# Keys of the first block handled in two stages, and the last four windows of turned keys split by VectorE

## The reference, cut to what matters

```python
q = layernorm(x) @ Wq + bq                      # 1024 x 128
k, v = ctx @ Wk + bk, ctx @ Wv + bv             # 6404 x 128
x = x + tanh(g_xattn) * softmax(q @ k.T / sqrt(128)) @ v
n = layernorm(x)
w = softmax(n @ Wr + br); keep the two largest of 8, divide by their sum
x = x + tanh(g_ffn) * sum_e w_e * (relu(n @ W1_e + b1_e) @ W2_e + b2_e)
```

## Time and profile before

| what | us |
|---|---|
| median of three executions | 283.12 |
| lowest and highest | 281.38, 283.39 |
| the profiled execution, its own time | 283.62 |
| span of its profile | 281.5 |
| TensorE busy | 269.8 |
| VectorE busy | 208.7 |
| ScalarE busy | 187.9 |
| GpSimd busy | 112.2 |

### The profile page before, as it was taken

How to read it: one execution, slowest core, us unless ns; L and a number is a source line. 1 busy time by engine, 2 the same in 40 slices (tenths; PEclk the granted TensorE clock), 3 DMA queues, 4 the chain that set the end, 5 groups by cost and what they waited for, 6 DMA issues and landing times.

```text
span 281.5 us, 5083 instructions
## 1 busy us (share of the span) xinstructions
PE 269.8 (96%) x1667; PEld 247.4 (88%) x1667; DVE 208.7 (74%) x415; ACT 187.9 (67%) x339; POOL 112.2 (40%) x147
## 2 busy tenths in 40 slices
PE   7988999999999999999999799998999899999994
PEld 7765899999999999999899799997899798999994
DVE  4795789966378987889737578777587688466796
ACT  2891665556566665565667698887554655799991
POOL 3796799647700020000000643870015443457530
PEclk9997999999999999999999999999999999999999
DMA  6600002000089100000000222344300111214212
GB/s 202 250 0 2 0 3 77 2 0 0 2 234 338 36 0 2 1 0 3 0 0 2 68 81 77 113 121 136 99 20 21 37 31 29 87 36 105 78 46 84
DMA packets 18485, 17.08 MB, mean 61 GB/s; under 512 B 2410, under 2 KB 14940, under 8 KB 18460
## 3 DMA queue, kind: packets, MB, share of 16 engines
q1 hardware_dynamic: 17372, 15.31, 17.9%
q0 software_dynamic: 640, 1.31, 1.7%
q10 hardware_dynamic: 448, 0.14, 0.2%
HBM read 13.34 MB, written 3.42 MB: 60 GB/s over the span
## 4 chain that ended last, share of the span: by engine, by line
PE 55%; issue 23%; DVE 10%; POOL 6%; DMA 3%; ACT 2%; POOLq 0%; DVEq 0%; ACTq 0%
DVE pmax L910 5%; PE ps L1265 4%; PE ps L1354 4%; PE ps L1355 4%; PE ps L1356 4%; PE ps L1332 4%; PE ps L1333 4%; PE ps L1334 4%; POOL x_slots L649 3%; PE ps L1213 3%; PE ps L1442 3%; PE ps L1467 2%; PE ps L1469 2%; PE ps L1468 2%; PE ps L1506 2%
## 5 line engine op out<-in xcount | busy, mean ns | idle before, releaser
L817 ACT ACTIVATE ex_hi<-ps 128x768 fp32r<-128x768 f32 (+1 forms) x78 | 57.0, 730 | 60.8 <-PE ps L1334 60.0
L1100 DVE TENSOR_TENSOR ex_lo<-ps,ex_hi 128x768 fp32r<-128x768 f32 (+2 forms) x67 | 59.1, 882 | 27.0 <-ACT ps L821 24.1
L910 DVE TENSOR_REDUCE pmax<-ps 128x1 f32<-128x512 f32 (+2 forms) x92 | 63.7, 731 | 12.8 <-PE ps L1265 11.8
L821 ACT ACTIVATE ps<-ps 128x768 f32<-128x768 f32 (+2 forms) x67 | 50.3, 750 | 0.0
L1332 PE MATMUL ps<-q_hi,ctxT_hi 97*128 97x384 f32 (+1 forms) x153 | 49.9, 326 | 0.0
L1354 PE MATMUL ps<-ex_hi,ctx_both 128*97 128x384 f32 (+1 forms) x153 | 49.8, 325 | 0.0
L1333 PE MATMUL ps<-q_lo,ctxT_hi 96*128 96x384 f32 (+1 forms) x153 | 49.1, 321 | 0.0
L1334 PE MATMUL ps<-q_hi,ctxT_lo 96*128 96x384 f32 (+1 forms) x153 | 48.7, 318 | 0.0
L1355 PE MATMUL ps<-ex_hi,ctx_both 128*96 128x384 f32 (+1 forms) x153 | 48.6, 318 | 0.0
L1356 PE MATMUL ps<-ex_lo,ctx_both 128*97 128x384 f32 (+1 forms) x153 | 48.6, 318 | 0.0
L547 POOL TENSOR_TENSOR rstd<-veps,minus_half 128x3 f32<-128x3 f32 (+1 forms) x6 | 5.0, 829 | 88.7 <-DVE veps L897 88.7
(11 more groups left out here) (212 smaller groups left out, 533.1 us busy)
## 6 DMA issues: line engine op xcount, KB each, us to landing
raw<-in_ctx_dram SPq DMA_DIRECT2D x6, 384.0 KB, 5.8
w_raw<-in_L_ffn_W_dram SPq DMA_DIRECT2D x8, 256.0 KB, 3.9
raw<-in_L_ffn_W_dram SPq DMA_DIRECT2D x8, 256.0 KB, 5.9
raw<-in_L_ffn_b_dram SPq DMA_DIRECT2D x8, 256.0 KB, 3.5
shared<-routing SPq DMA_DIRECT2D x8, 192.0 KB, 3.1
x_slots<-shared SPq DMA_DIRECT2D x1, 1088.0 KB, 6.3
y_slots<-shared SPq DMA_DIRECT2D x17, 64.0 KB, 1.5
shared<-in_L_ffn_b_dram SPq DMA_DIRECT2D x1, 512.0 KB, 3.5
```

The source lines that it names most:

```text
L817: nc.scalar.activation(ex_pair(ex_hi, u % P_RING, js, n), scores, ACT.Exp)
L821: nc.scalar.activation(whole, scores, ACT.Exp).then_inc(ex_ready, 1)
L910: nc.vector.tensor_reduce(pmax[:, FIRST_TILE[b] + t, place:place + 1], max_home(s)[:, 0:w], AX.X, ALU.max).then_inc(max_reduced, 1)
L1100: nc.vector.tensor_tensor(ex_pair(ex_lo, u % P_RING, js, n), whole, ex_pair(ex_hi, u % P_RING, js, n).bitcast(F32), ALU.subtract).then_inc ...
```

## The change

The maxima of block 0 are found in two stages. Stage one covers the first 3072 keys: 6 slots of 1024 keys at the start, and units 0 to 11 use the row of their maxima. The other 3332 keys make 14 slots of 512 keys (the last two of 260) beside units 2 to 9 of block 0; the second row is the maximum of those keys and zero, is kept in a copy of the query (`q_second`) and used by units 12 to 25. The slots of block 1 move to units 10 to 23 of block 0. The sums of stage two go to the other half of the bank; both halves are projected in turn (two more matmuls, in unit 7 of block 1), and VectorE joins them with the factor exp(`drop`), where `drop` is the difference of the two rows. The steps behind move by one or two units. Windows 9 to 12 of the turned keys (chunks 36 to 50) are turned behind the first slots into banks 5, 6, 7 and 5, copied once by ScalarE and split by VectorE from PSUM. GpSimd's order changes, and it makes the low part of exp for units 14 to 25. The transposes whose results are not read around `turn_max(0)` are gone.

```diff
-WARM_MAX = 12
-WARM_ROW = 5
...
-POST_FIRST = dict(u_copy=3, project=5, gate=5, residual=6, stats=7, turn=12, logits=14, shift=15, compare=16, exp=17,
+POST_FIRST = dict(u_copy=3, project=5, first_copy=6, project_second=7, gate=7, residual=8, stats=9, turn=13, logits=14, shift=15, compare=16, exp=17,
...
-POOL_LO_FROM = 15
+POOL_LO_FROM = 14
+
+STAGE_UNITS = 12
+SECOND_ROW_UNIT = 11
+TURNED_BY_VECTOR = 9
...
+    STAGE_KEY = 2 * STAGE_UNITS * P
...
+    PASS = [2 * BANK] + [BANK] * (ROUNDS - 1)
...
+    SLOTS = [(r, t, key, min(PASS[r], ROUND_KEYS[r][1] - key), ROUND_AT[r] + w)
+             for r in range(ROUNDS) for w, key in enumerate(range(*ROUND_KEYS[r], PASS[r])) for t in range(BLOCK_TILES[ROUND_BLOCK[r]])]
+    SLOTS_UNTIL = [sum(PLACES[k] * BLOCK_TILES[ROUND_BLOCK[k]] for k in range(r + 1)) for r in range(ROUNDS)]
...
+    ROUND_UNITS = {1: (0, 2, SECOND_ROW_UNIT - 2), 2: (0, SECOND_ROW_UNIT - 1, MAX_UNIT), 3: (1, 0, MAX_UNIT)}
...
+        for r, (block, first, last) in ROUND_UNITS.items():
+            if block == b and first <= i <= last:
+                n, units = SLOTS_UNTIL[r] - SLOTS_UNTIL[r - 1], last + 1 - first
+                return range(SLOTS_UNTIL[r - 1] + (i - first) * n // units, SLOTS_UNTIL[r - 1] + (i - first + 1) * n // units)
+        return []
+
+    def round_of(b, i):
+        return b + 1 if b or i >= STAGE_UNITS else 0
...
-        QK_UNIT = {1: 0, 2: 6}
+        QK_UNIT = {1: 2, 2: 6}
         TURN_X_UNIT = {2: 4}
-        SPLIT_UNIT = {1: 2, 2: 7}
-        ROWS_UNIT = 9
...
+        def window_bank(w):
+            return ps[:, [5, 6, 7, 5][w - TURNED_BY_VECTOR] if w >= TURNED_BY_VECTOR else w % 4, :]
...
+        def row_bank(r):
+            return UB[1] if r == 1 else MPAIR[:, 0, :]
...
-            last = (NW - 1) * BANK
+            last = TURNED_BY_VECTOR * BANK
...
+            inverse_deviation(2)
+            normalize(2)
+            split_ctx(1)
...
-            split_ctx(1)
-            inverse_deviation(2)
-            normalize(2)
...
-            for w in range(9, NW):
+            for w in range(7, TURNED_BY_VECTOR):
                 split_ctxT(w)
             for g in range(3, NG):
                 split_ctx(g)
+
+            for u in POOL_LO:
+                js = unit_chunks(u)
+                n = width(0)
+                pool.wait_ge(ex_ready, u + 1)
+                pool.wait_ge(ex_used, u - P_RING + 1)
+                nc.gpsimd.tensor_tensor(ex_pair(ex_lo, u % P_RING, js, n), ex_whole(u, js, n),
...
-            copy_ctxT_hi(NW - 1)
-            copy_ctxT_whole(NW - 1)
+            copy_ctxT_hi(TURNED_BY_VECTOR - 1)
+            copy_ctxT_whole(TURNED_BY_VECTOR - 1)
             copy_x(1)
+            for w in range(TURNED_BY_VECTOR, NW - 1):
+                copy_ctxT_hi(w)
...
+                if i == 1:
+                    copy_ctxT_hi(NW - 1)
+                if i == 3:
+                    nc.scalar.copy(q_second[0:C, :], q_hi[0:C, span(0)].bitcast(F32)).then_inc(q_second_ready, 1)
...
+                    n_u = n if b else 2 * n
+                    nc.scalar.copy(u_sb[:, 0:n_u], UB[b % 2][0:CA, 0:n_u]).then_inc(u_copied, 1)
+                if step_at(b, i, "first_copy"):
+                    act.wait_ge(first_projected, 1)
+                    nc.scalar.activation(first_share, UB[0][:, N0 * (HID + 1):N0 * (HID + 2)], ACT.Exp)
+                    nc.scalar.copy(first_proj, UB[0][:, 0:N0 * (HID + 1)].rearrange("p (t h) -> p t h", h=HID + 1)).then_inc(first_copied, 1)
...
-            def finish_max(b):
-                dve.wait_ge(max_reduced, SLOTS_UNTIL[b])
-                nc.vector.tensor_reduce(nmax[:, tiles(b)], pmax[:, tiles(b), 0:PLACES[b]], AX.X, ALU.max,
+            def finish_max(r):
+
+                ts = tiles(ROUND_BLOCK[r])
+                dve.wait_ge(max_reduced, SLOTS_UNTIL[r])
+                nc.vector.tensor_reduce(nmax[:, ts], pmax[:, ts, ROUND_AT[r]:ROUND_AT[r] + PLACES[r] + (1 if r == 1 else 0)], AX.X, ALU.max,
                                         negate=True).then_inc(nmax_ready, 1)
 
...
+            def row_max(r):
+
+                b = ROUND_BLOCK[r]
+                dve.wait_ge(max_row, r + 1)
+                row = q_second[C:CA, :] if r == 1 else q_hi[C:CA, span(b)]
+                ins = nc.vector.tensor_tensor(row, row_bank(r)[C:CA, 0:width(b)], q_hi[C:CA, span(b)].bitcast(F32), ALU.add)
+                ins.then_inc(row_ready, 1)
+                if r == 1:
+                    dve.wait_ge(row_ready, 2)
+                    nc.vector.tensor_tensor(drop[C:CA, :], q_second[C:CA, :].bitcast(F32), q_hi[C:CA, span(0)].bitcast(F32),
+                                            ALU.subtract).then_inc(drop_ready, 1)
+
+            def split_window(w):
+                js = window_chunks(w)
+                keys = slice(js[0] * P, js[0] * P + len(js) * P)
+                dve.wait_ge(ctxT_hi_ready, w + 1)
+                nc.vector.tensor_tensor(ctxT_lo[0:C, keys], window_bank(w)[0:C, 0:len(js) * P], ctxT_hi[0:C, keys].bitcast(F32),
+                                        ALU.subtract).then_inc(ctxT_lo_split, 1)
...
+            for w in range(TURNED_BY_VECTOR, NW - 1):
+                split_window(w)
...
+                    if b == 0:
+                        for t in range(nt):
+                            last = nc.vector.scalar_tensor_tensor(out=proj[:, t, :], in0=first_proj[:, t, :], scalar=first_share[:, t:t + 1],
+                                                                  in1=proj[:, t, :], op0=ALU.mult, op1=ALU.add)
...
-                        row_max(b + 1)
+                        row_max(b + 2)
+                    if b == 0 and i == SECOND_ROW_UNIT:
+                        dve.wait_ge(q_second_ready, 1)
+                        row_max(1)
...
+                    if b == 0 and i == 1:
+                        split_window(NW - 1)
+                    if b == 0 and i == SECOND_ROW_UNIT - 2:
+                        finish_max(1)
                     if b + 1 < NB and i == MAX_UNIT:
-                        finish_max(b + 1)
+                        finish_max(b + 2)
...
-                if w >= 4:
+                if 4 <= w < TURNED_BY_VECTOR:
                     pe.wait_ge(ctxT_f_ready, w - 3)
+                elif w + 1 == NW:
+                    pe.wait_ge(ctxT_lo_split, 1)
+                elif w >= TURNED_BY_VECTOR:
+                    pe.wait_ge(max_reduced, SLOTS_UNTIL[0] - (1 if w == TURNED_BY_VECTOR else 0))
...
-                if b and s <= SLOTS_UNTIL[b - 1] + 1:
-                    pe.wait_ge(row_ready, b)
+                if r in (1, 3) and s <= SLOTS_UNTIL[r - 1] + 1:
+                    pe.wait_ge(row_ready, r)
+                if r == 1 and s <= SLOTS_UNTIL[0] + 1:
+                    pe.wait_ge(ctxT_lo_split, NW - TURNED_BY_VECTOR)
...
-            def turn_max(b):
...
+                if r == 1:
+                    pe.wait_ge(q_lo_ready, NB)
                 for t in range(BLOCK_TILES[b]):
                     ft = FIRST_TILE[b] + t
-                    last = nc.tensor.matmul(MPAIR[C:CA, 0, t * P:(t + 1) * P], nmax[:, ft:ft + 1], ident[:, :],
...
             for s in range(SLOTS_UNTIL[0]):
                 score_for_max(s)
                 w = 4 + s
-                if s % 2 and w < NW:
+                if s % 2 and w < TURNED_BY_VECTOR:
                     turn_window(w - 1)
                     turn_window(w)
-                if s == NW - 5:
-                    turn_window(NW - 1)
-                if s == NW - 3:
-                    pe.wait_ge(ctxT_f_ready, NW - 3)
-                    turn_x(0, 1, x_home(1))
-            keep_warm(WARM_MAX, UB[1])
+            turn_window(TURNED_BY_VECTOR - 1)
+            pe.wait_ge(ctxT_f_ready, TURNED_BY_VECTOR - 3)
+            turn_x(0, 1, x_home(1))
+            turn_window(TURNED_BY_VECTOR)
             turn_max(0)
-            keep_warm(WARM_ROW, UB[1])
+            for w in range(TURNED_BY_VECTOR + 1, NW - 1):
+                turn_window(w)
...
+                if i == 1:
+                    turn_window(NW - 1)
+                if i == SECOND_ROW_UNIT:
+                    turn_max(1)
                 if i == ROWS_UNIT:
                     pe.wait_ge(w_consts_in, 8 * 16)
-                    pe.wait_ge(q_lo_ready, NB)
+                    pe.wait_ge(row_ready, 2)
...
-                if i == 0:
-                    pe.wait_ge(row_ready, b + 1)
...
+                q = q_second[:, :] if round_of(b, i) == 1 else q_hi[:, span(b)]
                 if u < 2:
-                    pe.wait_ge(ctxT_f_ready, NW)
...
-                    nc.tensor.matmul(dst, ctxT_hi[0:CA, keys], q_hi[:, span(b)], start=True, stop=False)
...
-                dst = UB[b % 2]
+                stage = round_of(b, i) == 1
+                dst = UB[b % 2][:, n:2 * n] if stage else UB[b % 2][:, 0:n]
+                first, final = {0: (0, 2 * STAGE_UNITS - 1), 1: (2 * STAGE_UNITS, NC - 1)}.get(round_of(b, i), (0, NC - 1))
                 wait_lo(pe, u)
```

(14 more changed lines are left out.)

101 lines of the change are left out of this document (53 added, 48 removed).

## The result

The changed kernel took 292.3 us (median of 4 executions, 291.0 to 292.5), the kernel before 282.5 beside it (4 executions): ratio 1.034, 95% interval 1.029 to 1.039. It is slower, as forecast, but by 9.8 us (9.6 by the ratio) and not by 4: 292.3 lies outside the range of 280.5 to 290.5. The profiled execution took 292.18 us with a span of 290.4, so the comparison of the two traces has 8.9 us of span to explain (290.4 - 281.5). Some executions in the experiments were over 1.5% longer than the shortest of the same kernel, at a lower mean clock, and the ratios leave these out.

A forecast was written before the change was run, and what follows sets the result against it. TensorE was taken as the bound, except at the start, where VectorE's reductions were. Start -9.0, block 0 +12.3 and block 1 +0.55 gave +3.8 on 283.62, 287.4; it said 287.2 us, own range 285.0 to 289.5, with rivals 280.5 to 290.5.

The forecast's parts named there:

- the stall: Block 0, three-slot units: third matmul waits for a reduction; 0.71 us in ten units (7.1), unit 23 0.55, unit 11 0.6.
- the start: Up to block 0's unit 3: fewer reductions and transposes before the first scores; gain 9.0 us (7 to 9.8).
- block 0 from unit 3 on: Block 0 up to block 1's scores: moved maxima, extra turn and waits together cost 12.3 us.
- block 1: Block 1: second projection 0.36 and two one-column matmuls for `drop` 0.2 add 0.55 us on a full TensorE.
- Before: 33.58: Scores of block 0's unit 3: profiled start in the kernel before, set against the forecast 24.6.
- Maxima and `turn_max(1)`: Block 0 behind unit 3: 16 more maximum matmuls cost 3.6 us, four more small turn matmuls 0.5.
- TensorE is ready after 0.47: Three-slot unit: TensorE is ready for the third matmul 0.47 us behind the first; it can start only at 1.18.
- Removed from here: nothing: Block 0 from unit 3: nothing goes but one unit's low part, moved from VectorE to GpSimd, hidden on both.
- moved here from unit 0: Unit 2 of block 0: block 1's folded query, about 0.35 us of TensorE work, now comes before unit 3's scores.
- Carried to the end: Behind block 1: everything depends on TensorE's order, so the difference stays to the end, +3.8 us.
- Rival 3: Behind the start or in the staged part: clock falls to 1.2 GHz; one or two falls give 289 to 292; 0.12.
- Rivals 1, 2 and 4: Stall absent or nearly filled (279.1; 0.15); half as long (283.7; 0.15); VectorE's start queue longer (289.2; 0.08).

The follow-up runs named there:

- before24: The kernel before, with the first two turned slots in units 24 and 25 of block 2 in place of 23 and 24: ratio 1.002.
- after24: The changed kernel, with the first two turned slots in units 24 and 25 of block 2 in place of 23 and 24: ratio 1.031.
- late_third: The changed kernel, with the third maximum matmul of block 0's three-slot units issued behind values: ratio 1.0045 to the kernel before.
- crowded: The kernel before, with only block 1's slots put into units 10 to 23 in place of 1 to 23: ratio 1.034.
- crowded_late: The kernel before, with block 1's slots in units 10 to 23 and a unit's third maximum matmul behind values: ratio 1.005.
- turn5: The changed kernel, with block 2's x turned in unit 5 in place of unit 4: ratio 1.0365 to the kernel before.
- after_again: The changed kernel unaltered, measured again in the second set: 298.39 us, ratio 1.026 to the kernel before.
- both: The changed kernel, with the third maximum matmul behind values and block 2's x turned in unit 5: 290.33 us, ratio 0.998 to the kernel before.
- best24: The changed kernel: third maximum behind values, block 2's x in unit 5, eight transposes in unit 1, drop in unit 22, first slots in units 24 and 25: ratio 0.999.

## Why the prediction was wrong

The direction was right and the stall that decides it too; the size was not: +9.8 in place of +4. Where the difference comes from is best read between two executions whose clock stayed at 1.00 up to the slot matmul, `before24` and `after24`, which are the kernels before and after up to the end of block 2. Three terms of the sum were mis-sized: the start gained 6.8 (31.76 to 25.00) for 9.0, block 0 from unit 3 on cost 15.0 (42.94 to 57.92) for 12.3, and block 1 cost 1.2 for 0.55. Together that is +9.4, the difference at unit 23, in place of +3.8. In the pair of profiles with the rows above the sum at the slot matmul is about the same (+9.67), but by luck: the start gained 1.9 more there, since the clock had fallen in the profile before, and 2.3 were lost again at the late load.

- **The start (-9.0).** Right: -8.7. Unit 0's scores at 18.87 for 19.1, `finish_max` at 17.29 to 17.45 for 17.55, `turn_max` 0.60 at full clock, a split from PSUM 0.63 (1.88 for three) for 0.6, scores of unit 2 at 22.49 for 22.6. The step that failed is "Before: 33.58": it took one execution for the kernel. 1.8 of those 33.58 are a clock fall, 0.53 in the earlier trace rows, that the profiled execution of before had and `before24` has not, so the change gains 6.8 where neither clock falls. The profile's 283.62 was above all four executions beside the changed kernel too (281.38 to 283.39); I took off 0.5, and it was 1.1 over their median.
- **Maxima and `turn_max(1)` (+3.6, +0.5).** They agree with the stretch: 3.6 + 0.5, the stalls' 9.7 and unit 4's 1.1 make 14.9, which is what was measured. No run has them alone.
- **The stall (7.1 + 0.55 + 0.6).** The kind is shown three times: it goes with the third matmul's place (`late_third`), comes in the kernel before with one number (`crowded`) and goes again (`crowded_late`). The term was mis-sized: 0.82 in a unit, not 0.71. The start of the third matmul was right (1.19 for 1.18 behind the first); the failing step is "TensorE is ready after 0.47", which prices the third at 0.235 although TensorE starts it from idle; it costs 0.34. Nine plain units then make 7.4, unit 11 1.6 for 1.31, unit 23 0.69 for 0.55: 9.7 in place of 8.25.
- **"Removed from here: nothing"; the folded query "moved here from unit 0".** This is the step that had the mechanism wrong. I moved the query's products and priced them, but not what follows them: its low part is made on VectorE in unit 3, and the turn of block 2's x in unit 4 needs the bank that it reads. I never asked who waits for the moved split. 1.1 us; `turn5` takes 1.05 of it away.
- **Block 1 (0.55).** 1.13. The second projection was right (0.37). The two matmuls for `drop` were put at 0.2, at most 0.4, by their single column. They took 0.53, and the first projection ahead of them 0.17 more than before:

```profile
95.53 0.61 PE L1457 MATMUL ps<-wv_sb,u_sb 97*128 97x129 f32 x4
96.06 0.60 PE L1464 MATMUL ps<-ctxT_hi,drop 1*128 1x1 f32 x4
96.59 0.42 PE L1445 MATMUL ps<-ex_hi,ctx_both 128*97 128x384 f32 x1
```

  Each float32 matmul shows as two records, so four records are 0.13 each with one column, as `turn_max`'s are with 128.
- **"Carried to the end".** True within block 2, up to its unit 23, within 0.02 us. Behind it 2.3 came on top at the wait for x_slots, and 0.7 came back in the expert stages. The wait stood in the profile of before (1.0), I had not weighed it. By `after24` and `after_again` the 2.3 are the execution's and not the change's. What gave 0.7 back stays open.
- **Rival 3, the clock.** Wrong for the staged part: over 24.9 to 82.8 us, with 11 waits for reductions in it, the granted clock was 1.00 (busy 50.59 of 57.90):

```profile
24.90:82.80 57.90, 50.59 (x344) 42.58 (x342) 42.69 (x72) 26.22 (x52) 32.26 (x28) 1.00 0.03 10
```

  Right for the poor stretch behind the start in some executions: of the seven traces of kernels with the changed start and no added transposes five have a granted clock of 0.50 to 0.57 in a stretch between 22 and 28 us, those of `after` and `after24` not. The Trainium skill (TensorE: Matmul & The Clock Gate, "A second HAM failure mode: psum-queue depth-cycling") warns, by a bf16 kernel, that short idle turns at PSUM banks lose throughput to the clock. In this kernel the short turns did not, at 0.55 us idle in 2.95; what preceded a fall was a longer poor stretch (1.98 us idle at 202, 0.50 behind it).
- **Rivals 1, 2 and 4.** No, by the units: the stall is whole, and VectorE's queue at the start was as forecast. The band within 1% has 0.20 in one place of the forecast and 0.22 in another; 0.22 is what its parts give.

## What to carry to other kernels

When a change packs work more densely beside a full engine, go through one unit of it in program order and ask which instruction now waits within the unit, and what stands behind it in the queue. Here a third use of a two-deep ring cost 0.82 us each time before `values` and 0.1 behind them; ordering was worth 7 us, and the two stages, with the order right, came out about even (`both` 0.998 and, measured again, 1.006; `best24` 0.999). A unit loses more than the bracket says (0.82 for 0.55), so measure such a stall from start to start. When a producer is moved, follow its consumer and the buffers it holds, not only its own cost. And a profile is one execution: where its clock has fallen once, compare with a second one before the fall is counted as something to gain.
